# A transformer kernel's mixture stage: from two groups of 16 token tiles, one tile at a time, to three groups of 8, 12 and 12, two tiles at a time

## The reference, cut to what matters

```python
h = jax.nn.gelu(xf @ wg1 + bg1, approximate=False)
logits = (h @ wg2 + bg2)[:, :E]
probs = jax.nn.softmax(logits, axis=-1)
top_vals, top_idx = jax.lax.top_k(probs, K)            # E = 20, K = 2
gates = jnp.zeros((N, E)).at[jnp.arange(N)[:, None], top_idx].set(top_vals)
# per expert: y = y + gates[:, e, None] * (xf @ We[e] + be[e])
x = _layernorm(x + y)                                  # x itself is the layernorm of the scan's output
```

## Time and profile before

| | us |
|---|---|
| median of 3 runs | 2891.48 (2886.39 to 2901.14) |
| the profiled execution | 2889.74 |
| its span, first to last instruction | 2888.0 |
| mean granted TensorE clock, share of full | 0.941 |
| busy in the span: PE, DVE, ACT, POOL | 2566.3, 1988.2, 1359.1, 1071.4 |
| moved by DMA | 158.49 MB, mean 55 GB/s |

### The profile page before, as it was taken

How to read it: one execution, slowest core, us unless ns; L and a number is a source line. 1 busy time by engine, 2 the same in 40 slices (tenths; PEclk the granted TensorE clock), 3 DMA queues, 4 the chain that set the end, 5 groups by cost and what they waited for, 6 DMA issues and landing times. The chain is left out here.

```text
span 2888.0 us, 43799 instructions
## 1 busy us (share of the span) xinstructions
PE 2566.3 (89%) x14918; PEld 1580.3 (55%) x14918; DVE 1988.2 (69%) x4117; ACT 1359.1 (47%) x2458; POOL 1071.4 (37%) x1061
## 2 busy tenths in 40 slices
PE   8699999999999999979999997899999999954971
PEld 4343333333333333336777775688888888842861
DVE  4577666676666676426666754999999999973345
ACT  2035555555555555634445443655555555531220
POOL 0112222222222221111001000699998999934434
PEclk9779999999999999989999998999999999976985
DMA  5722222222333330030000000000000000022864
GB/s 184 190 53 53 53 53 53 53 53 53 59 60 59 60 65 13 1 101 15 15 22 23 15 8 9 22 11 11 11 11 15 11 11 11 4 83 69 268 206 124
DMA packets 100605, 158.49 MB, mean 55 GB/s; under 512 B 14948, under 2 KB 65432, under 8 KB 97240
## 3 DMA queue, kind: packets, MB, share of 16 engines
q1 hardware_dynamic: 87592, 133.00, 18.6%
q0 software_dynamic: 6144, 16.79, 1.8%
q10 hardware_dynamic: 6704, 6.56, 0.7%
HBM read 95.04 MB, written 56.77 MB: 53 GB/s over the span
## 5 line engine op out<-in xcount | busy, mean ns | idle before, releaser
L645 ACT ACTIVATE ssm_in_dt<-att_s 128x512 f32<-128x512 f32 (+3 forms) x1280 | 616.4, 534 | 531.0 <-PE att_s L544 307.9
L679 DVE TENSOR_REDUCE att_partmax<-att_s 128x1 f32<-128x512 f32 x768 | 491.4, 684 | 257.6 <-PE att_s L530 222.0
L518 PE MATMUL att_s<-att_ks,att_qs 49*128 49x512 f32 (+3 forms) x1280 | 518.9, 461 | 67.4 <-DVE att_partmax L679 39.2
L544 PE MATMUL att_s<-att_qs,att_ks 49*128 49x512 f32 (+3 forms) x1280 | 467.7, 431 | 7.7 <-ACT ssm_in_dt L645 5.5
L1719 POOL TENSOR_TENSOR ssm_cc<-ssm_cc,ssm_h 128x512 f32<-128x512 f32 x256 | 332.5, 1299 | 248.2 <-DVE ssm_h L1775 246.6
L544 PEld LDWEIGHTS att_s<-att_qs,att_ks 49*128 49x128 f32 x1280 | 215.4, 187 | 372.7 <-ACT ssm_in_dt L645 269.3
L485 POOL TENSOR_SCALAR_AFFINE_SELECT ssm_in_dt<-ssm_in_dt 128x256 f32<-128x256 f32 x256 | 104.5, 408 | 791.0 <-ACT ssm_in_dt L645 786.5
L587 PE MATMUL att_o_ps<-ssm_in_dt,att_vst 128*32 128x512 f32 (+3 forms) x2560 | 348.6, 553 | 3.5 <-ACT ssm_in_dt L645 3.4
L1734 POOL TENSOR_TENSOR ssm_out_z<-ssm_out_z,ssm_cc 128x512 f32<-128x512 f32 x256 | 336.2, 1313 | 0.1
L518 PEld LDWEIGHTS att_s<-att_ks,att_qs 49*128 49x128 f32 x1280 | 229.1, 192 | 148.9 <-DVE att_partmax L679 104.1
L1671 ACT ACTIVATE ssm_cc<-ssm_c_ps,ssm_cur 128x512 f32<-128x512 f32 x256 | 199.2, 778 | 226.4 <-PE ssm_c_ps L1626 226.4
(11 more groups left out here) (297 smaller groups left out, 4139.8 us busy)
## 6 DMA issues: line engine op xcount, KB each, us to landing
moe_sorted<-att_hidden SPq DMA_DIRECT2D x26, 512.0 KB, 9.0
moe_rows<-moe_sorted SPq DMA_DIRECT2D x52, 256.0 KB
moe_answers<-moe_mixed SPq DMA_DIRECT2D x52, 256.0 KB
att_far<-bias_tables SPq DMA_DIRECT2D x96, 136.0 KB, 8.0
att_stage_q<-qk_halves SPq DMA_DIRECT2D x96, 128.0 KB, 4.3
att_stage_k<-qk_halves SPq DMA_DIRECT2D x96, 128.0 KB, 7.1
qk_halves<-qkv_high SPq DMA_DIRECT2D x16, 512.0 KB, 5.8
qk_halves<-qkv_low SPq DMA_DIRECT2D x16, 512.0 KB, 5.8
```

The lines of the kernel that those rows point to most:

```text
L518: mm = nc.tensor.matmul(s1[:, S1_BANK[at], 0:hi - lo], qs[p % 3][half(b, ROWS), I * P:(I + 1) * P], ks[p % 3][half(b, ROWS), lo:hi], start ...
L544: mm = nc.tensor.matmul(s2[:, turn % RING, 0:hi - lo], ks[p % 3][half(b, ROWS), J * P:(J + 1) * P], qs[p % 3][half(b, ROWS), lo:hi], start ...
L645: nc.scalar.activation(prob[:, b, step % 2, x * CH + lo:(x + 1) * CH], s2[:, turn % RING, 0:CH - lo], ACT.Exp, scale=1.0 / HD).then_inc(s2 ...
L679: nc.vector.tensor_reduce(most, piece, AX, ALU.max).then_inc(s1_read, 1)
```

## The change

1. **Three groups** of 8, 12 and 12 token tiles, with sorted lists of 36, 44 and 44 tiles: 124 sorted tiles in place of 104. The blank stores become 31 (9, 11 and 11), two per head of the attention.
2. **Order.** The first group is gated alone (chunks 0 and 1). The second (chunks 2 to 4) is gated beside the first group's 16 scatters. The third (chunks 5 to 7) is gated inside the first group's sorted tiles, with its steps at fixed pairs `p`. The second group's 24 scatters are held to pairs 0 to 14, the third group's 24 to pairs 15 to 33.
3. **Pairs.** `turn_rows`, `read_rows`, `experts` and `read_y` each handle two sorted tiles with one wait and one copy of 512 columns. The turned rows go through `z_ps`, the answers fill whole banks of `y_ps`. PE turns pair `p + 2` ahead of the experts of pair `p`.
4. **ACT reads the answers** of the first 18 pairs (`BY_SCALAR`), DVE those of the other 44, with a semaphore each.
5. **SP** stores first and loads second.
6. **Combining** runs inside the loop for 20 token tiles, from pair 36 on, and after it for 12.
7. The memset of `be_pad` moves from POOL to DVE, and `prepare`, which splits the biases, to a later place.

```diff
-LIST = 52
+GROUP_LIST = (36, 44, 44)
+GROUP_TILES = (8, 12, 12)
+PAIR_FIRST = (0, 18, 40)
+BY_SCALAR = GROUP_LIST[0] // 2
+COMBINED = [36 + 5 * n // 4 for n in range(GROUP_TILES[0])] + [47 + 5 * n // 4 for n in range(GROUP_TILES[1])]
...
         @block.sync
...
+            def load(p):
+                h = group_of_pair(p)
+                n = p - PAIR_FIRST[h]
                 if n == 0:
-                    eng.wait_ge(scattered[h], 16 * 2 * HT)
-                after(eng, turned, 2 * (g - 3))
+                    eng.wait_ge(scattered[h], 16 * 2 * GROUP_TILES[h])
+                after(eng, turned, p - 3)
...
+            def store(p):
...
+                read_of(eng, p + 1)
...
-            for g in range(2 * GROUP):
-                if g + AHEAD < 2 * GROUP:
-                    load(g + AHEAD)
-                store(g)
+            for p in range(AHEAD):
+                load(p)
+            for p in range(PAIRS_ALL):
+                store(p)
+                if p + AHEAD < PAIRS_ALL:
+                    load(p + AHEAD)
...
         @block.gpsimd
...
+            scatter(0, 0, 0)
+            scatter(1, 0, 14)
+            scatter(2, 15, 18)
+            for h in range(NG3):
+                gather(h)
...
         @block.tensor
...
+            def turn_rows(p):
+                eng.wait_ge(rows_loaded[p % 4], 16 * (p // 4 + 1))
+                if p < 2:
+                    eng.wait_ge(z_copied, NT // 2)
+                after(eng, rowsT_ready, p - 1)
                 for j in range(2):
                     for k in range(KT):
+                        mm = nc.tensor.transpose(z_ps[:, p % 2, (j * KT + k) * P:(j * KT + k + 1) * P], rows[p % 4][:, j, k * P:(k + 1) * P], ident[:])
                 mm.then_inc(turned, 1)
...
+            def experts(p, at):
+                eng.wait_ge(rowsT_ready, p + 1)
+                if p == 0:
+                    eng.wait_ge(spot_read, 1)
+                read_of(eng, p - 1)
+                for j in range(2):
+                    y = y_ps[:, p % 2, j * D:(j + 1) * D]
+                    for k in range(KT):
+                        nc.tensor.matmul(y, rowsT[p % 3][:, j, k], w[:, k, ds(at[j], D)], start=k == 0, stop=False)
+                    mm = nc.tensor.matmul(y, three[:], be_pad[:, ds(at[j], D)], start=False, stop=True)
+                mm.then_inc(y_ready, 1)
...
             turn_rows(0)
+            at, then = columns(0), None
+            turn_rows(1)
+            for p in range(PAIRS_ALL):
+                if p == 2:
+                    turn_x(5)
+                if p == 3:
+                    hide(5)
+                    turn_x(6)
+                if p == 5:
+                    logits(5)
+                    hide(6)
+                    turn_x(7)
+                if p == 7:
+                    logits(6)
+                    hide(7)
+                if p == 9:
+                    logits(7)
+                if p == 14:
+                    count(2)
...
+                if p + 2 < PAIRS_ALL:
+                    turn_rows(p + 2)
+                experts(p, at[2 * (p % 2):2 * (p % 2) + 2])
...
         @block.scalar
...
+            def read_y(p):
+                eng.wait_ge(y_ready, p + 1)
+                after(eng, mixed_stored[p % 4], 16 * (p // 4))
+                nc.scalar.copy(mixed[p % 4][:].rearrange("p j d -> p (j d)"), y_ps[:, p % 2]).then_inc(y_read_act, 1)
...
+                if p + 2 < PAIRS_ALL:
+                    read_rows(p + 2)
+                if p < BY_SCALAR:
+                    read_y(p)
...
         @block.vector
...
+            choose(0)
+            normalise(2)
+            settle(0)
+            normalise(3)
+            read_x(2)
+            means(4)
+            read_x(3)
+            normalise(4)
+            means(5)
+            prepare()
+            list_tiles(0)
+            read_x(4)
+            means(6)
+            choose(1)
+            normalise(5)
+            settle(1)
+            list_tiles(1)
...
+            for p in range(BY_SCALAR, PAIRS_ALL):
+                read_y(p)
```

More of the change, by code:

```diff
@@ L2035, in experts @@
[L2035 to L2054 removed]
+                eng.wait_ge(dve_set, 5)
@@ new lines, in count @@
+                tiles = GROUP_TILES[h]
+                total = count_bank(h)[:, 0:(tiles + 1) * E2].rearrange("p (n e) -> p n e", e=E2)
+                nc.tensor.matmul(total, earlier[:], both[:, 0:tiles + 1], start=True, stop=False)
+                for n in range(tiles):
+                    mm = nc.tensor.matmul(total[:, n + 1:], all_ones[:], both[:, n:n + 1, :].to_broadcast([P, tiles - n, E2]),
+                                          start=False, stop=n == tiles - 1)
+                mm.then_inc(spot_ready, 1)
@@ L2101, in read_rows, with spread @@
-            def read_rows(g):
-                eng.wait_ge(turned, g + 1)
-                after(eng, y_ready, g - 2)
-                nc.scalar.copy(rowsT[g % 3][:], xT_ps[:, g % 2, 0:D].rearrange("p (k n) -> p k n", k=KT)).then_inc(rowsT_ready, 1)
+                    nc.scalar.copy(x3[:, 2 * at:2 * at + 2], z_ps[:, at % 2].rearrange("p (j d) -> p j d", j=2)).then_inc(z_copied, 1)
+            def spread(c):
+                eng.wait_ge(var_ready, c + 1)
+                tiles = slice(TPC * c, TPC * (c + 1))
+                nc.scalar.activation(std[:, tiles], mv[:, tiles, 1], ACT.Sqrt, bias=eps[:]).then_inc(std_ready, 1)
@@ new lines, in _ @@
+            copy_x(0)
+            copy_x(1)
+            gelu(0)
+            gelu(1)
+            spread(2)
+            spread(3)
+            copy_z(4)
+            exponent(0)
+            copy_z(5)
+            copy_z(6)
+            copy_z(7)
+            copy_x(2)
+            spread(4)
+            copy_x(3)
+            gelu(2)
+            copy_x(4)
+            gelu(3)
+            gelu(4)
+            spread(5)
+            spread(6)
+            exponent(1)
+            read_rows(0)
@@ new lines, in choose @@
+            def choose(h):
+                tiles, first = GROUP_TILES[h], GROUP_FIRST[h]
+                eng.wait_ge(lg_ready, (first + tiles) // TPC)
+                p = pr[:, 0:tiles]
+                step(nc.vector.tensor_tensor(p, lg_ps[:, 0:tiles * E2].rearrange("p (n e) -> p n e", e=E2), along(b2[:], tiles), ALU.add))
+                step(nc.vector.tensor_reduce(red[:, 0:tiles], p, AX, ALU.max))
+                nc.vector.tensor_tensor(p, p, over(red[:, 0:tiles], tiles), ALU.subtract).then_inc(shifted, 1)
@@ L2209, in settle @@
             def settle(h):
+                tiles, length = GROUP_TILES[h], GROUP_LIST[h]
                 eng.wait_ge(spot_ready, h + 1)
-                total = y_ps[:, h, 0:(HT + 1) * E2].rearrange("p (n e) -> p n e", e=E2)
-                step(nc.vector.tensor_scalar(number[:], total[:, HT], float(P - 1), None, ALU.add))
+                total = count_bank(h)[:, 0:(tiles + 1) * E2].rearrange("p (n e) -> p n e", e=E2)
+                step(nc.vector.tensor_scalar(number[:], total[:, tiles], float(P - 1), None, ALU.add))
```

479 lines of the change are left out of this document (246 added, 233 removed).

## The result

The changed kernel takes **3169.39 us**, median of 4 runs (3166.59 to 3174.31), against 2895.18 us for the kernel before in its 4 runs (2886.39 to 2901.14): ratio **1.0952**, 95% interval 1.0917 to 1.0986. The profiled execution took 3166.59 us, its span is 3164.8.

The account below looks back on a forecast made before the run. The prediction saw 122 us of mostly idle gating and 161 us of sorted tiles with PE busy for 139. It summed 2889.7 - 55 + 394 - 10 = 3219, rounded to 3220 us, range 3050 to 3310.

Parts of the forecast that it names:

- the ring: Sorted-tile loop: store, load behind it, landing, waiting turn, then next experts run in series; loop 556 us, +394 us.
- Its period: Time per pair in the loop: 4.4 + 0.25 + 0.6 + 0.43 + 3.2 = 8.9 us, in place of 3.1.
- The loop: Sorted tiles, first to last pair: 543 + 5 + 8 = 556 us in place of 161.7, +394 us.
- The 13 us for the third group's gating and for the gather burst: Extras in the loop: 5 us excess for gating inside pairs, 8 us for 12 gathers issued in a burst.
- Start: Start of sorted tiles moves from 2667.3 to 2612, a gain of 55 us, with 7 us of wait included.
- DVE beside scatters: Second group's gating beside the first group's scatters: nothing charged; the skill's rule would make the start 29 us later.
- Gathers behind the last store: After the last store, 24 gathers in place of 32, each 1.23 us with its gap: -10 us.
- Ring at full clock: Rival in the loop: clock recovers in each pair, period 6.8 us, loop 425, total 3088; chance 0.20.
- No ring: Rival in the loop: loads in time, tiles PE-bound, loop 168 us, total 2831; chance 0.04.
- Slow landing: Rival in the loop: each load takes 5.33 us, period 11.0 us, total 3345; chance 0.09.
- The long wait at the start: Rival: scatters hold up second group's gating by 34 us in place of 7, total 3246; chance 0.08.
- What the regrouping alone offers: Whole kernel if loads were in time and tiles PE-bound: total 2831 against the profiled execution's 2889.7.

Follow-up runs that it names:

- e1: Changed kernel with SP issuing load(p + 3) ahead of store(p); 2886.73 us, ratio 1.0127.
- e2: Changed kernel, store still first, with PE and ACT turning one pair ahead in place of two; 2888.16 us, ratio 1.0132.
- e3: Changed kernel with load ahead of store and loads five pairs ahead in place of three; 2824.84 us, ratio 0.991.
- e5: Changed kernel with 8 extra matmuls, result unread, ahead of each turn from pair 8 on; 3083.46 us, ratio 1.0657.
- e9: Changed kernel, unchanged, run again on a third chip; 3171.25 us, ratio 1.1122.
- e8: Kernel before, unchanged, profiled again on a third chip; 2851.26 us in its one run.
- e11: Changed kernel with load first and five pairs ahead, run again on a third chip; 2825.76 us, ratio 0.9915.
- e6: Changed kernel with load first, five pairs ahead, and the first group's scatters held to four under way; 2865.24 us, ratio 0.9899.
- e7: Kernel before with its first group's 32 scatters held to four under way; 2891.99 us, ratio 1.0016.

## Why the prediction was right, point by point

Against the spans: 2888.0 before, - 56.5 at the start (2667.4 to 2610.9), + 349.3 in the loop (2610.9 to 3121.8, 510.9, in place of 161.6), - 16.0 behind the last store (59.0 to 43.0) gives 3164.8. The forecast had - 55, + 394 and - 10: 3220, which is 51 us or 1.6% too much.

- **SP's new order: the ring.** Right, and shown, by e1 and e2, which open it from its two sides, and by e3, which removes it and 345 us with it (3171.25 to 2825.76 on one chip). PE waited 58 times for its rows; store and load are 0.41 us apart; the DMA share is 0.28.
- **Its period.** Foretold 8.9 us; the pair shown takes 9.09, the mean is 8.55. By parts in that pair: PE and the way to the copy 4.99 us in place of 4.4 + 0.25; copy, store and load issue 1.13 in place of 0.6 + 0.43, with DVE's copy of 0.69; the landing 2.97 in place of 3.2. I said that the clock would recover a little within a pair. In the pair shown it does not; in about half of the pairs the second tile's four matmuls take less than at the low clock (1.92 us), down to 1.03, and the mean clock of the loop is 0.71, just over the 0.5 to 0.7 foretold. The Trainium skill, TensorE: Matmul & The Clock Gate, section HAM oscillation — how this bites in real kernels, has such a loop start every step at the low clock. 54 of 59 turns agree with it, 0.95 to 1.12 us where 0.66 is full clock. The other five are those of pairs 4, 5, 7, 9 and 16, and each stands right behind a piece of the third group's gating on PE. The 9.2 us of the prediction took the pair for slow to its end as well, and that the mean of 8.55 does not bear out.
- **The loop, 45 us too long.** This is the term that was mis-sized. 59 loads are issued inside it, so 58 steps, not 60, carry the period: 2 x 8.9 = 17.8. The period itself: 58 x 0.35 = 20.3. The 13 us for the third group's gating and for the gather burst came on top in the forecast, but are inside the mean. The gating had the wrong sign: it stood in time in which PE waited, and the turns right behind it ran at full clock, as behind e5's fills, so that the steps beside it are the shortest of the loop (7.8 us, the rest 8.7). The two steps beside the gather burst are the longest, 9.73 and 9.94 us. Against these stand 15.2 us for the ends of the loop (3.1 to the first load, 12.1 behind the last) where I had 9.3. 17.8 + 20.3 + 13 - 5.9 = 45.2.
- **Start, - 55.** Right, 56.5, but in part by luck, with three errors in its reasons. Row numbers were ready near 2575.4 and not 2579.5, 4 us sooner. From the first scatter to the experts the sum had 24.6 us with no wait, and the changed kernel takes 30.0 where there is none (e9): the second group's `count` stands on PE ahead of the first turn, and its gating ends later than the first loads. That is 5 us the other way. And I took the sum of the earlier trace rows, 34 us, as waits beside scatters, where the first of the two links is DVE's own work. The 7 us that I put in for such a wait was 4.6 us: 34.6 from first scatter to experts with it, 30.0 without. On chips that have no such waits the start gains only 35.8 us (2650.2 in e8, 2614.4 in e11).
- **DVE beside scatters: nothing charged.** Right. DVE is busy for 9.28 of 10 us and 15 steps of scatters take 19.99 us, 1.33 each in place of 1.28. One of them took 1.46 us in place of 0.96, while DVE filled `passed` (L2362) from two operands in SBUF, and so did the first of the second group's (1.53 us). The Trainium skill, SBUF — State Buffer, section Who interferes with whom, says that a DVE instruction with two inputs in SBUF contends with a GpSimd instruction that reads SBUF; all that the trace shows of it is 0.8 us over the 15 steps. The page's rule for two-port modes, which the prediction held against the earlier trace rows, is not tested by that window: most of DVE's work there is statistics, and the `tensor_scalar` that normalises takes as long for 256 columns as they do, so that no faster mode shows:

```profile
2602.37 1.37 DVE L2163 BATCH_NORM_STATS2 moe_stats<-moe_x 128x6 f32<-128x256 f32 x4
...
2604.30 1.39 DVE L2177 TENSOR_SCALAR moe_x<-moe_x,moe_mv,moe_rstd 128x256 f32<-128x256 f32 x4
```

- **Gathers behind the last store: - 10.** With its gap each takes (22.9 + 6.4) / 24 = 1.22 us by the groups of lines, as foretold (1.23). The tail gave 16 us back all the same, since the kernel before had waits in its own: without them (e8 to e9) it shortens by 10.9 us, 53.7 to 42.8.
- **The rivals.** "Ring at full clock" was 3088, and with the clock held up e5 measures 3083.46. That it is so near is partly luck: e5's 58 steps of 7.03 us come to the same 408 us as the 60 of 6.8 foretold. "No ring" was 2831 in total, a loop of 168 us; e3 has the loop at 166. Slow landing did not come: 3.7 us at most among the 15 landings that the profile of the changed kernel holds, 4.0 among all 62 of e9. The long wait at the start did not come either, though there was a piece of it, 4.6 us.
- **What the regrouping alone offers.** I put it at 59 us. With the ring gone it is 25 us on one chip (2849.35 to 2824.84) and 21 on another (2847.25 to 2825.76). By the spans of e8 and e11, 2849.6 and 2822.9: - 35.8 at the start, + 18.8 in the loop (144.4 to 163.2, 20 more tiles), - 9.7 behind it, - 26.7 in all. The trace that I predicted from has both the start and the loop of the kernel before lengthened by waits (160.4 us from the first to the last matmul of the experts, where e8 has 144.4), and I had counted them as part of the kernel. On the chip with waits e6 wins 45.0 us at the start over e7 and then has 198.0 us of loop to e7's 156.4; its ratio is 0.990 all the same.

The best version is e3's (measured again as e11): 0.991 and 0.9915 of the kernel before.

## What to carry to other kernels

For each in-order queue, write down what stands ahead of the step whose wait you add, and follow it round. If the walk comes back one step later, the sum along it is the period of a step, and buffers that are already full don't help (the changed kernel: 8.55 us). If it comes back two steps later, two steps share the sum (e1, e2: 3.7 us each). The cure here was to put the issue that waits for nothing ahead of the one that waits, and then to give it the lead that its landing needs when the queues are full. And a wait that the chain calls "another core or an unknown queue" may belong to the chip or the hour of the trace and not to the kernel, so profile the old kernel on a second chip before you price an edit by it.

## What the runs showed that I had not expected

- Two classes of batches, each on its own chip. While POOL issues a row of indirect DMAs, other engines stand still for long in some of them (in e7 24.72 us before one ACT instruction, 16.88 on DVE, 15.21 on PE) and not in others (2.63 us before the same ACT instruction in e8), with the same spacing of 1.28 to 1.29 us between scatters. It is worth some 40 us of the kernel before. By the spans of before and e8 that is 25.5 us at the start, 16.0 in the loop and 5.3 behind it, less 8.3 by which the layers ahead are quicker where the waits are. In the changed kernel nothing of it shows in the total (3169.39 and 3171.25 us): 4.6 us at the start stand against the same 8 us ahead.
- It is not a pile of scatters under way: there are never more than four. The Trainium skill, Runtime: NRT & Kernel Launch, section Instruction fetch mechanics, says that an engine's sequencer fetches its code in blocks over a DMA queue of its own. The traces speak against that as the stall: in e7 the queues of kind "instruction" move nothing between 2602 and 2660, around the whole wait of 24.72 us (2616.7 to 2641.4), and the one block of the changed kernel's 8.11 us wait starts at 2591.93 and takes 0.51 us. The cause is open.
- A load of 256 KB lands in 2.7 to 4.0 us, median 2.9, when it is alone with one store (e9), and in 2.7 to 7.3 us, median 4.1, in the full loop of e3, which is nonetheless the fastest.
- Eight idle matmuls per pair, 1.9 us of work, take 86 us off a loop that waits for its data. They shorten nothing in the wait; they keep the granted clock of what follows it at 0.97 in place of 0.71. The third group's gating does the same, unasked, for the pairs beside it.
